# Other shares of the dequantisation levels for three stages of a four-layer kernel on one core

## The chip, the cores and the metric

The kernel runs on one core of a Trainium2 chip. The metric is the device time of that core in microseconds (us), the median of several executions. The profile is of one execution, with its own time.

## The reference

The input x is 64 sequences of 32 positions and 512 features, float32. Four layers follow, each `x = x + ffn(cond(x))`:

- Layer 0: a long convolution along the features with a kernel made from state-space parameters, masked by a length, then a product with a 512x512 fp8 weight.
- Layer 1: every sequence is multiplied by one of 16 adapters (512x512, chosen by `itok_B_1_14`), then a gated feed-forward net of hidden width 1376: `silu(x w1') * (x w2')`, times `w3'`. The three weights are first quantised and dequantised.
- Layers 2 and 3: routed low-rank products, a small memory with top-8 selection, a gate, a convolution across positions and a last 512x512 product.

What the change is about is the quantisation in layer 1. In blocks of 64 elements:

```
absmax = max(abs(block)); idx = searchsorted(bounds, block / absmax)   # 15 bounds
weight = NF4_CODE[idx] * absmax
```

## The kernel before, in words

All products are float32 on TensorE; activations lie transposed (512 features as 4 chunks of 128 partitions, 2048 tokens in 4 blocks `tb` of 512 columns). Each engine has its own instruction list, written out by hand, and the engines wait for each other by semaphores. So the order of the work on an engine is the order of the code.

**Dequantisation.** The weights are cut into 15 units (`UNITS`): 11 units of w1 and w2 together (128 rows by 1024) and 4 of w3 (128 by 1408). A unit takes 15 levels, one for each bound, so there are `PARTS` = 225 levels, numbered m; unit u has levels 15u to 15u+14. ScalarE (ACT) compares the raw weights with bound i (L761) and writes one of four `above` buffers; it may run `NAB` = 4 levels ahead of VectorE. VectorE (DVE) adds the step to the unit's accumulator (L1605 for the first level, L1608 for the others). After a unit's last level DVE multiplies by the block maxima (L1614), then TensorE transposes the unit (`turn_unit`, L1029) and ACT copies it out of PSUM (`evac_quant`, L769). Before level 5 of a unit, DVE prepares the next one (`start_unit`: L1579 maxima, L1580 to L1586 normalising). The raw weights of unit u+2 are loaded by SyncE (SP) once ACT has done with unit u (L519 to L526).

**Where the levels run.** They fill gaps between other work of ACT and DVE, by tables that say how many levels have been done after each step: `K_CONV` (16 steps of the convolution), `K_FFN0` (16 products of layer 0, `NF0` levels), `K_AD` (16 adapters, `NAD` levels) and `K_UP` (44 up products of layer 1). Before a step's own work both engines run the levels of its share. Tables before: 8 levels in the convolution, 7 in layer 0's product, 53 among the adapters (3 or 4 each), 154 in the up projection (97 of these in its first 24 steps, so that the units of w1 and w2 are done there), and `LATE` = 3 at the end.

**The work around them.** In layer 0's product TensorE makes 16 products (`p_ffn0`); DVE adds each to X (L1685). After the last one (`d_x1` = 16) DVE, ACT and GpSimd (POOL) copy X into Y, sequences in order of their adapter (L1690, L789, L683, L687). Then TensorE turns unit 0 and goes through the adapters: 22 groups of up to 4 sequences here, each 32 matmul instructions, with the numbers of groups 0, 1, 1, 2, 2, 1, 1, 2, 1, 2, 2, 1, 1, 2, 3, 0 for the adapters 0 to 15; ACT copies each group out (L801), and a group may start only when the group four before it is out. The first up product needs all groups out. `turns_ad` and `turns_up` say after which adapter or up product a unit is turned; both are worked out from the tables. SP loads the weights of adapter a when adapter a-4 is done, and in the last four turns also stores X (`keep`).

In the up projection a product n gives two banks; ACT takes them out (silu and copy, L836, L837; for the last chunk L840, L841), POOL or DVE multiply them (L691; `hidden`, L1706, L1707). Product n waits until product n-2 is out. For four products (`AHEAD`: n = 28, 29, 32, 33) DVE runs `hidden(n)` before the levels of step n.

Of the kernel before, what the change touches and what calls it, by code (L numbers as in the profile page):

```python
# [32 lines left out]
ADAPT = 16  # L33
# [61 lines left out]
def build(nc, A, out):  # L95
    ctx = ExitStack()
    with ctx:
# [259 lines left out]
        for n in """l_zq g_xs a_xs d_nrm m_ready m_used g_nrm d_xs a_rk a_v2 p_rke a_kk g_pad d_wz p_va a_va p_lgt a_lgt l_l3 a_w16 d_ak d_rmx g_x2 l_cst l_s4 l_s5 l_w0 l_u l_x l_len l_ids l_kpz l_kp0 l_kp1 l_kp2 l_kp3 l_dsk g_dsk d_kz l_keep l_back l_strip0 l_strip1 l_strip2 l_strip3 l_strip4 l_raw0 l_raw1 l_wa0 l_wa1 l_wa2 l_wa3 l_late l_prep l_l3w l_aim g_dec g_c p_c10 d_mix a_out1 a_up g_h  # L357
# [13 lines left out]

        LEV = len(BOUNDS)
        PARTS = LEV * NU
        NCV, NF0, NAD, LATE = 8, 7, 53, 3
        UP_A, UP_B = 24, 20
        BANKS0 = [4, 5, 0, 1, 2, 3]
        BANKS_ST = [3, 2, 5, 3]
# [10 lines left out]
        K_CONV = [min(max(g - 1, 0) * 2 // 3, NCV) for g in range(HG)]  # L388
        K_FFN0 = [K_CONV[-1] + (NF0 + NCV - K_CONV[-1]) * (n + 1) // (TB * DC) for n in range(TB * DC)]
        AD_LAST = K_FFN0[-1] + NAD  # L390
        K_AD = [K_FFN0[-1] + (a + 1) * NAD // ADAPT for a in range(ADAPT)]
        W12 = LEV * NH
        K_UP = [AD_LAST - (-(W12 - AD_LAST) * (n + 1) // UP_A) if n < UP_A else
                min(W12 - (-(PARTS - LATE - W12) * (n + 1 - UP_A) // UP_B), PARTS - LATE) for n in range(TB * NH)]
        assert K_UP[-1] == PARTS - LATE and K_AD[-1] == AD_LAST

# [15 lines left out]
        def parts_of(K, i, first=0):  # L412
            return range(K[i - 1] if i else first, K[i])

        def units_between(a, b):

            return [u for u in range(NU) if a < LEV * (u + 1) <= b]

        def turns_ad(a):
            return units_between(K_AD[a - 3] if a >= 3 else K_FFN0[-1], K_AD[a - 2]) if a >= 2 else []  # L420

        def turns_up(n):
            late = units_between(K_AD[-2], PARTS - LATE)
            at = {u: next(i for i in range(TB * NH) if K_UP[i] >= LEV * (u + 1)) + (1 if u >= NU - 2 else 2) for u in late}
            return [u for u in late if min(at[u], TB * NH - 1) == n]
# [63 lines left out]
        def _(sp):  # L489
# [26 lines left out]
            def load_unit(u):  # L516
                kind, c = UNITS[u]
                if u >= 2:
                    sp.wait_ge(s["m_ready"], 15 * (u - 1))  # L519
                    sp.wait_ge(s[f"l_raw{u % 2}"], 32 * (u // 2))  # L520
                slot = raw[:, u % 2, :]
                got = s[f"l_raw{u % 2}"]
                if kind == 1:
                    h = HCH[c]
                    sp.dma_start(slot[0:h, 0:D], A["w1"][c * P:c * P + h, :]).then_inc(got, 16)
                    sp.dma_start(slot[0:h, D:2 * D], A["w2"][c * P:c * P + h, :]).then_inc(got, 16)  # L526
                else:

                    g, q = c // 2, c % 2
                    o = q * (2 * HID - HALF)  # L530
                    for k in range(2):
                        cols = slice(k * HALF // 2, (k + 1) * HALF // 2)
                        sp.dma_start(slot[:, cols], A["w3"][g * P:(g + 1) * P, o + cols.start:o + cols.stop]
                                     ).then_inc(got, 16)
# [28 lines left out]
            def keep(tb):  # L563
                sp.wait_ge(s["d_x1"], TB * DC)
                sp.dma_start(xkeep.ap()[:, :, tok(tb)], X[:, :, tok(tb)]).then_inc(s["l_keep"], 16)
# [19 lines left out]
            for a in range(NWS - 1, ADAPT):  # L585
# [5 lines left out]
                else:  # L591
                    done = sp.value_load(order[0:1, NB + a - NWS + 1:NB + a - NWS + 2], min_val=0, max_val=NGR)
                    sp.wait_ge(s["p_ad"], done + 1)
                    sp.wait_ge(s[f"l_wa{a % NWS}"], WSINC[a % NWS] * (a // NWS))
                    for u in units_between(K_AD[a - NWS - 1] if a > NWS else K_FFN0[-1], K_AD[a - NWS]):
                        load_unit(u + 2)
                load_adapter(a)
                if a >= ADAPT - TB:
                    keep(a - ADAPT + TB)
            for u in units_between(K_AD[-1 - NWS], PARTS):  # L600
                if u + 2 < NU:
# [119 lines left out]
        def _(act):  # L721
# [32 lines left out]
            def level(m):  # L754

                u, i = divmod(m, LEV)
                h, w = unit_shape(u)
                normed(act, u)
                if m >= NAB:
                    act.wait_ge(s["m_used"], m - NAB + 1)  # L760
                nc.scalar.activation(above[0:h, m % NAB, 0:w], raw[0:h, u % 2, 0:w], ACT.Relu,  # L761
                                     scale=STEEP, bias=cst[0:h, C_BND + i:C_BND + i + 1]).then_inc(s["m_ready"], 1)
# [30 lines left out]
            for a in range(ADAPT):  # L793
                for k in parts_of(K_AD, a, K_FFN0[-1]):
                    level(k)
# [1292 lines left out]
```

## Time and profile before

| what | value |
|---|---|
| median of 3 runs | 868.88 us |
| the runs | 865.85, 868.88, 873.6 us |
| the profiled execution | 865.41 us |
| its span | 863.6 us |
| TensorE busy | 825.8 us, 96% of the span |
| VectorE busy | 638.9 us, 74% |
| ScalarE busy | 415.8 us, 48% |
| granted TensorE clock | 1.000 |

The profiled execution's own time is 1.8 us above its span (what lies around the first and the last instruction), and a little under the lowest of the three runs. The three runs lie 7.75 us apart, 0.9% of the time. A line such as L1608 is a line of the kernel. L969 is the helper of nearly all matmuls, so they are told apart by their operands. A float32 matmul stands as two records.

### The profile page before, as it was taken

What the parts mean: (1) busy time and instruction counts of PE and PEld (TensorE: products, weight loads), DVE (VectorE), ACT (ScalarE), POOL (GpSimd) and SP (SyncE); (2) the same over time, 40 slices, a digit from 0 to 9 for tenths busy, and PEclk for the clock granted to TensorE, in tenths of its full rate; (3) what the DMA queues carried; (4) which work ended last, traced back from release to release, by engine and by line L of the source; (5) the groups of instructions that cost most, each with busy time, mean ns of one, the idle gap of its engine ahead of it and who ended that gap; (6) DMA issues with size and microseconds to landing.
All of it is one profiled execution on the core that took longest, in us unless ns stands there. A gap on an engine that the chain in (4) does not pass through costs nothing.

```text
span 863.6 us, 10782 instructions
## 1 busy us (share of the span) xinstructions
PE 825.8 (96%) x3325; PEld 459.6 (53%) x3326; DVE 638.9 (74%) x981; ACT 415.8 (48%) x550; POOL 152.7 (18%) x162
## 2 busy tenths in 40 slices
PE   2499899999999999999999999999999999999998
PEld 2498799984444444444344444444455554543443
DVE  7899799969999999998999986343362462458445
ACT  5055188869787787886788730000011232245100
POOL 4100099101122211121122200002402022020000
PEclk9999999999999999999999999999999999999999
DMA  6696157920000001101010030013020000002022
GB/s 208 222 375 226 56 214 229 325 106 24 24 3 23 25 18 35 34 0 35 1 33 0 1 97 1 0 58 138 0 68 1 1 0 1 1 1 50 0 98 98
DMA packets 35151, 61.06 MB, mean 71 GB/s; under 512 B 6170, under 2 KB 8988, under 8 KB 34460
## 3 DMA queue, kind: packets, MB, share of 16 engines
q1 hardware_dynamic: 34232, 60.32, 20.6%
q0 software_dynamic: 352, 0.04, 0.2%
q8 instruction: 26, 0.43, 0.2%
q14 instruction: 25, 0.20, 0.1%
q10 hardware_dynamic: 516, 0.07, 0.0%
HBM read 50.90 MB, written 8.47 MB: 69 GB/s over the span
## 4 chain that ended last, share of the span: by engine, by line
PE 83%; DVE 8%; POOLq 3%; issue 2%; POOL 2%; ACT 1%; DMA 1%; SPq 0%; ACTq 0%; DVEq 0%
PE ps L969 81%; DVE acc L1608 3%; POOLq L685 2%; POOL Yp L687 1%; PE ps L1029 1%; PE ps L1301 1%; DVE W2T L1474 1%; DVE T L1608 1%; DVE W2T L1468 1%; DMA T<-kpad 0%; DVE W2T L1471 0%; DMA W2T<-in_log_dt 0%; DVE raw L1586 0%; DVE amax L1579 0%; POOLq L687 0%
## 5 line engine op out<-in xcount | busy, mean ns | idle before, releaser
L761 ACT ACTIVATE above<-raw,cst 128x1024 uint8<-128x1024 f32 (+2 forms) x225 | 267.8, 1233 | 48.6 <-DVE T L1608 20.0
L1608 DVE SCALAR_TENSOR_TENSOR acc<-above,acc 128x1024 f32<-128x1024 uint8 (+2 forms) x112 | 159.6, 1425 | 14.7 <-ACT above L761 11.4
L969 PE MATMUL ps<-Up,W2T 128*128 128x512 f32 (+1 forms) x404 | 160.6, 593 | 0.0
L969 PE MATMUL ps<-Up,W1T 128*128 128x512 f32 x344 | 155.5, 594 | 2.6 <-DVE Up L1707 2.2
L1608 DVE SCALAR_TENSOR_TENSOR T<-above,T 128x1024 f32<-128x1024 uint8 (+1 forms) x84 | 129.4, 1540 | 3.4 <-ACT above L761 0.5
L969 PEld LDWEIGHTS ps<-Up,W2T 128*128 128x128 f32 (+1 forms) x404 | 66.5, 177 | 86.4 <-issue 86.4
L969 PEld LDWEIGHTS ps<-Up,W1T 128*128 128x128 f32 x344 | 64.1, 190 | 81.6 <-issue 76.3
L969 PE MATMUL ps<-Yp,W3T 128*128 (+3 forms) x618 | 104.5, 322 | 1.6 <-POOL Yp L683 1.2
L969 PEld LDWEIGHTS ps<-Yp,W3T 128*128 128x128 f32 (+1 forms) x618 | 79.2, 192 | 23.1 <-issue 22.5
L969 PE MATMUL ps<-X,W3T 128*128 128x512 f32 (+2 forms) x184 | 78.7, 579 | 0.0
L969 PE MATMUL ps<-X,W2T 128*128 128x512 f32 x140 | 61.3, 594 | 0.0
L969 PEld LDWEIGHTS ps<-X,W3T 128*128 128x128 f32 (+1 forms) x184 | 34.1, 190 | 42.6 <-issue 41.0
L1748 DVE TENSOR_TENSOR Yp<-Yp,ps 128x512 f32<-128x512 f32 x14 | 9.3, 684 | 54.0 <-PE ps L969 53.9
L969 PE MATMUL ps<-Up,W3T 128*128 128x256 f32 (+4 forms) x202 | 45.6, 381 | 0.0
L969 PEld LDWEIGHTS ps<-X,W2T 128*128 128x128 f32 x140 | 26.3, 190 | 31.9 <-issue 31.6
L687 POOL COPY Yp<-X x44 | 40.9, 981 | 1.7 <-issue 1.7
L969 PE MATMUL ps<-W1T,W2T 128*128 128x512 f32 (+1 forms) x144 | 36.0, 436 | 4.8 <-DVE W2T L1551 4.8
L691 POOL TENSOR_TENSOR Yp<-Yp 128x512 f32<-128x512 f32 x13 | 18.8, 1442 | 118.8 <-ACT Yp L837 118.8
L711 POOL TENSOR_TENSOR X<-X,Yp 128x2048 f32<-128x2048 f32 x4 | 18.1, 4528 | 121.8 <-ACT Yp L890 121.8
L969 PEld LDWEIGHTS ps<-Up,W3T 128*128 128x128 f32 (+1 forms) x202 | 32.0, 191 | 12.3 <-issue 11.0
L691 POOL TENSOR_TENSOR X<-X,Yp 128x512 f32<-128x512 f32 x15 | 23.5, 1565 | 79.0 <-ACT X L837 79.0
L1901 DVE TENSOR_TENSOR Up<-Up,ps 128x512 f32<-128x512 f32 x4 | 2.8, 688 | 40.6 <-PE ps L1258 40.6
(344 smaller groups left out, 977.1 us busy)
## 6 DMA issues: line engine op xcount, KB each, us to landing
W3T<-in_wa SPq DMA_DIRECT2D x8, 1024.0 KB, 7.2
raw<-in_w SPq DMA_DIRECT2D x20, 256.0 KB, 3.0
W3T<-kpad SPq DMA_DIRECT2D x9, 512.0 KB, 8.5
Up<-in_xconv SPq DMA_DIRECT2D x4, 1024.0 KB, 8.7
X<-in_xT SPq DMA_DIRECT2D x4, 1024.0 KB, 9.7
W1T<-in_wa SPq DMA_DIRECT2D x4, 1024.0 KB, 7.6
xkeep<-X SPq DMA_DIRECT2D x4, 1024.0 KB, 10.6
X<-xkeep SPq DMA_DIRECT2D x4, 1024.0 KB, 9.4
```

Of the source, the lines that this page charges most:

```text
L685: bs = [pool.value_load(order[0:1, bass.ds(t * 4 + i, 1)], min_val=0, max_val=NB - 1) for i in range(4)]
L687: pool.tensor_copy(Y[:, :, bass.ds(t * (4 * S) + i * S, S)], X[:, :, bass.ds(b * S, S)]).then_inc(s["g_xs"], 1)
L691: nc.gpsimd.tensor_tensor(slots[UPS[n]], slots[UPS[n]], sg[n % 2], ALU.mult).then_inc(s["g_h"], 1)
L711: nc.gpsimd.tensor_tensor(X[:, :, tok(tb)], X[:, :, tok(tb)], Y[:, :, tok(tb)], ALU.add).then_inc(s["g_xc"], 1)
L761: nc.scalar.activation(above[0:h, m % NAB, 0:w], raw[0:h, u % 2, 0:w], ACT.Relu, scale=STEEP, bias=cst[0:h, C_BND + i:C_BND + i + 1]).then ...
L969: return nc.tensor.matmul(o, l, r, start=start, stop=stop, **kw)
L1029: last = nc.tensor.transpose(dst, src, ident[0:h, 0:h])
L1301: last = nc.tensor.transpose(ps[:, BANKS_ST[t], c * P:(c + 1) * P], Y[:, c, tile(tb, t)], ident)
L1468: link(V.tensor_tensor(o, a, b, op))
L1474: link(V.scalar_tensor_tensor(out=o, in0=a, scalar=x, in1=b, op0=op0, op1=op1))
L1608: V.scalar_tensor_tensor(out=ac, in0=src, scalar=float(STEPS[i]), in1=ac, op0=ALU.min, op1=ALU.add).then_inc(s["m_used"], 1)
L1748: V.tensor_tensor(o, a, b, op).then_inc(s["d_mix"], 1)
```

## The change

The tables get other sizes. Layer 0's product takes 10 levels in place of 7. The adapters take 57 in place of 53: the first 12 share 41 evenly (3 or 4 each), the last four take 4, 4, 5 and 3. What is left for the up projection is 147 levels in place of 154: its first 24 steps take 90 in place of 97, and from step 23 on `K_UP` is as it was.

```
-        NCV, NF0, NAD, LATE = 8, 7, 53, 3
+        NCV, NF0, NAD, LATE = 8, 10, 57, 3
+        AD_END = [4, 4, 5, 3]
...
-        K_AD = [K_FFN0[-1] + (a + 1) * NAD // ADAPT for a in range(ADAPT)]
+        AD_EVEN = NAD - sum(AD_END)
+        K_AD = [K_FFN0[-1] + ((a + 1) * AD_EVEN // (ADAPT - 4) if a < ADAPT - 4 else AD_EVEN + sum(AD_END[:a + 5 - ADAPT]))
+                for a in range(ADAPT)]
```

Worked out from the tables: the shares in layer 0's product were 0 0 1 0 1 0 1 0 0 1 0 1 0 1 0 1 and are 0 1 0 1 1 0 1 1 0 1 0 1 1 0 1 1. Unit 0 was finished at product 15 and is finished at product 11. The shares among the adapters were 3 3 3 4 3 3 4 3 3 4 3 3 4 3 3 4 and are 3 3 4 3 4 3 3 4 3 4 3 4 4 4 5 3. Units 1, 2 and 3 were turned after the adapters 6, 11 and 15 and are turned after 5, 9 and 14. Units 4 to 9 were turned after the up products 3, 7, 10, 14, 18, 22 and are turned after 2, 5, 9, 13, 17, 21; later units as before.

## Rows read from the trace of the kernel before

**Rows 1.** The page: busy time of the engines, and the chain that ended last.
```profile
PE 825.8 (96%) x3325; PEld 459.6 (53%) x3326; DVE 638.9 (74%) x981; ACT 415.8 (48%) x550; POOL 152.7 (18%) x162
PE 83%; DVE 8%; POOLq 3%; issue 2%; POOL 2%; ACT 1%; DMA 1%; SPq 0%; ACTq 0%; DVEq 0%
```

**Rows 2.** Waits of PE, whole span: total us, times, longest us.
```profile
PE ps L969 <- DMA Yp<-in_l3aT: 14.6, 1, 14.6
...
PE ps L969 <- DVE Up L1707: 2.2, 1, 2.2
```

**Rows 3.** Timeline of DVE, end of layer 0's product: start, us.
```profile
102.57 0.75 DVE L1685 SCALAR_TENSOR_TENSOR X<-ps,wsc,X 128x512 f32<-128x512 f32 x1 [0.48 <-PE ps L969]
103.24 1.22 DVE L1608 SCALAR_TENSOR_TENSOR acc<-above,acc 128x1024 f32<-128x1024 uint8 x1
104.48 1.23 DVE L1614 TENSOR_TENSOR acc<-acc,amax 128x1024 f32<-128x1024 f32 x1
105.75 0.75 DVE L1685 SCALAR_TENSOR_TENSOR X<-ps,wsc,X 128x512 f32<-128x512 f32 x1
```

**Rows 4.** Timeline of PE at the same place.
```profile
105.77 1.09 PE L1029 MATMUL ps<-cst,acc 128*128 128x128 f32 x8 [1.43 <-DVE acc L1614]
108.06 4.48 PE L969 MATMUL ps<-Yp,W3T 128*128 x38 [1.21 <-POOL Yp L683]
```

**Rows 5.** Busy time by stretch: layer 0's product, the adapters.
```profile
74.00:105.00 31.00, 30.34 (x137) 24.92 (x135) 24.41 (x31) 9.93 (x10) 0.00 (x0) 1.00 0.34 119
...
109.00:190.00 81.00, 80.62 (x719) 80.19 (x719) 71.15 (x67) 64.09 (x74) 42.78 (x51) 1.00 0.66 228
```

**Rows 6.** Timeline of DVE among the adapters and behind them.
```profile
109.49 0.86 DVE L1605 TENSOR_SCALAR W2T<-above 128x1024 f32<-128x1024 uint8 x1 [1.03 <-ACT above L761]
...
115.62 1.22 DVE L1579 TENSOR_REDUCE amax<-raw 128x16 f32<-128x1024 f32 x1
...
118.84 12.57 DVE L1608 SCALAR_TENSOR_TENSOR W2T<-above,W2T 128x1024 f32<-128x1024 uint8 x10
...
179.05 0.69 DVE L1605 TENSOR_SCALAR acc<-above 128x1024 f32<-128x1024 uint8 x1
...
191.76 1.23 DVE L1608 SCALAR_TENSOR_TENSOR acc<-above,acc 128x1024 f32<-128x1024 uint8 x1 [6.95 <-ACT above L761]
```

**Rows 7.** Timeline of ACT, last group out and first up product out.
```profile
190.02 0.60 ACT L801 ACTIVATE Up<-ps x1 [2.98 <-PE ps L969]
190.52 4.26 ACT L761 ACTIVATE above<-raw,cst 128x1024 uint8<-128x1024 f32 x4
...
204.29 0.59 ACT L837 ACTIVATE Yp<-ps 128x512 f32<-128x512 f32 x1
```

**Rows 8.** Timeline of PE in the up projection and at its end.
```profile
204.94 3.70 PE L969 MATMUL ps<-Up,W1T 128*128 128x512 f32 x8 [0.26 <-ACT Yp L837]
...
428.35 3.70 PE L969 MATMUL ps<-Up,W1T 128*128 128x512 f32 x8 [2.16 <-DVE Up L1707]
...
508.97 1.39 PE L1029 MATMUL ps<-cst,acc 128*128 128x128 f32 x11 [0.70 <-issue]
```

**Rows 9.** Timeline of DVE around the products taken ahead, and the last unit.
```profile
398.22 0.68 DVE L1706 TENSOR_TENSOR Yp<-Yp,ps 32x512 f32<-32x512 f32 x1 [3.23 <-ACT Yp L841]
...
427.61 0.69 DVE L1707 TENSOR_TENSOR Up<-Yp,ps 64x512 f32<-64x512 f32 x1
...
502.27 4.94 DVE L1608 SCALAR_TENSOR_TENSOR acc<-above,acc 128x1408 f32<-128x1408 uint8 x3 [2.89 <-ACT above L761]
```

**Rows 10.** DMA: a load of raw weights by SP; the stores of X.
```profile
175.83 0.35 SPq L525 DMA_DIRECT2D raw<-in_w  x1
```
```profile
xkeep<-X SPq DMA_DIRECT2D x4, 1024.0 KB, 10.6
```

**Rows 11.** DVE groups by form: adapters (first), up projection (second).
```profile
L1608 DVE SCALAR_TENSOR_TENSOR acc<-above,acc 128x1024 f32<-128x1024 uint8 x15 | 18.4, 1225 | 1.8 <-ACT above L761 1.3
```
```profile
L1608 DVE SCALAR_TENSOR_TENSOR T<-above,T 128x1024 f32<-128x1024 uint8 x42 | 60.0, 1430 | 1.4
```

## The prediction

> **What bounds the kernel now.** I read the page first. TensorE is busy for 96% of the span, and the chain that ended last runs through it for 83% [rows 1]. The granted clock was 1.00 throughout. So time can only be won where TensorE waits, or where its matmuls start further apart than they need to, and it can be lost wherever it is made to wait anew. The view of PE's waits then says how much there is. The largest wait, 14.6 us, stands before the first matmul that needs a load at the very start and has nothing to do with the levels [rows 2]. From the convolution on none is longer than the 2.2 us for DVE's L1707 [rows 2]. The timelines of PE show where these waits are, and what else is near the stages that the change touches:
>
> - Before unit 0 is turned: 1.43 us, until L1614 is done; right behind it 1.21 us until X has been copied for the first group [rows 4].
> - Before the third up product: 0.26 us, for ACT's L837 [rows 8].
> - Before up product 34: 2.16 us, for DVE's L1707 [rows 8].
> - Before the last unit is turned: 0.70 us [rows 8].
>
> These make 5.8 us, 0.7% of the time, and that is all that any placing of the levels could bring. A busy DVE or ACT is no cost here by itself: DVE's 74% matters at those places alone.
>
> **Layer 0's product, three levels more.** The end of this stage is the first term. DVE adds product 14 to X at 102.57, then runs level 14 (1.22 us) and closes unit 0 with L1614 (1.23 us), and only at 105.75 adds product 15 [rows 3]. TensorE had finished product 15 at 105.77 - 1.43 = 104.34 [rows 4]. Two things hang on this: the turning of unit 0 (the 1.43 us), and the copies of X, which wait for all 16 additions. The turn, 1.09 us long, covers part of the second wait. What sets the first group's start at 108.06 is the addition at 105.75, 2.31 us before it [rows 3, 4].
>
> After the change, unit 0 is closed at product 11. Behind product 14's addition stands one ordinary level, m = 17, and no L1614. Adding product 15 can thus start at 102.57 + 0.67 + 1.24 = 104.5, if product 14 is not taken sooner; the steps in the rows are 103.24 - 102.57 = 0.67 and 104.48 - 103.24 = 1.24. Product 14's row has an idle time of 0.48 before it that ended with PE, so it can't be sooner. Because level 16 now stands before product 14 as well, and its predecessor has none, I allow 0.1 to 0.2 us on top of this: 104.6 to 104.7 against 105.75. The gain is 105.75 - 104.65 = **1.1 us**. The turn of unit 0 moves up by more than that and stops being felt.
>
> Is there room for the three levels? DVE is busy 24.41 us of the 31 us from 74 to 105 [rows 5]. Two of the added levels are of 1.24 us and one, the first of unit 1, is a cheaper L1605; together at most 3.7 us, against 6.6 us of idle time. ACT is busy 9.93 us of 31 [rows 5] and has room for three more. The load of unit 2's raw weights stays where it is in SP's order, before adapter 3, and what it waits for comes earlier. So this part costs nothing while there is cover; without the cover it would be 1.24 us a level. Six PSUM banks stand between TensorE and a late addition, so it takes a backlog of several products before that is felt.
>
> **Adapters, four levels more.** TensorE is busy 80.62 us of 81 here [rows 5]. The stage ends when its 22 groups are done and out; it does not wait for DVE. I follow DVE, because ACT may be only four levels ahead of it, and ACT's copying out of a group stands behind the levels of that adapter's share. A level takes 12.57 / 10 = 1.257 us, and preparing a unit 118.84 - 115.62 = 3.22 us [rows 6]. With the first level at 0.73 and closing at 1.26 a unit takes 0.73 + 14 x 1.257 + 3.22 + 1.26 = 22.8 us. DVE starts with m = 18 at about 108.3 (before, m = 15 at 109.49 [rows 6], less the 1.1 us). Two levels, a preparation, ten levels and the closing make 19.6 us, so unit 1 is done at 127.9, unit 2 at 150.7 and unit 3 at 173.5. Before, they were turned at 136.7, 167.0 and 189.5; now, after adapters 5, 9 and 14, at about 132, 154 and 188. The smallest reserve is about 3 us, at unit 2, so the moved turns cost nothing.
>
> The end of the stage is tighter. Adapter 14's share ends with m = 71, which ACT can make only when DVE has used m = 67. From 173.5: five levels of unit 4 (5.8), the preparation of unit 5 (3.2) and three levels (3.8) lead to 186.3. ACT's level takes 1.07 us (4.26 / 4 [rows 7]), to 187.4, and then two groups that have been waiting go out at 0.5 us each, to 188.4. TensorE, 1.1 us earlier than before, ends its last group at 189.5 - 1.1 = 188.4 and turns unit 3 until 189.3. The last group goes out meanwhile. So the reserve is about nothing. My formula for a unit gives 68.4 us for the three units of before, and DVE took 179.05 - 109.49 = 69.6 us for them [rows 6]. With half of this difference I put a new wait of **0.5 us** at the start of the up projection; its bounds are 0 (DVE as by the formula) and 2 us (DVE short by all of that difference, and a load arriving late, the rival below). Before, DVE stood idle for 6.95 us at this very place [rows 6], because ACT had its last four levels behind the last group, at 190.52 [rows 7]. These 6.95 us are what pays for the four levels on DVE, and they are why so little is lost.
>
> For SP, the loads of units 3, 4 and 5 move up by one to two adapters or so. In front of adapter 7's and adapter 11's weights SP now waits for the end of units 1 and 2 on ACT, by my count for 1 to 2 us. Those weights are needed 13 us or more after their issue; even a store of that size takes only 10.6 to land [rows 10], so this is covered.
>
> **Up projection, seven levels fewer.** Steps 0 to 23 have 90 levels in place of 97. The 0.26 us before the third product go: ACT has four levels ahead of product 0 instead of five, and those of adapter 15 are three, not four. It was done with L837 at 204.29 + 0.59 [rows 7]; two levels fewer are at least 2.1 us. Gain **0.3 us**. The rest of the seven levels comes off a DVE that no one waits for. At product 28 DVE is idle for 3.23 us until ACT has handed it the product [rows 9]. So whatever DVE is ahead by is lost there: it starts again at 398.22 (less the shift), with the same list of work, because `K_UP` is unchanged from step 23 on. The 2.16 us at product 34 arise only behind this point, from 398.22 to 427.61 + 0.69 without a pause to speak of [rows 8, 9]. They stay. The 0.70 us before the last unit stay too: DVE waits 2.89 us for ACT before its last three levels, and ACT for TensorE's last up product [rows 9].
>
> The rows also show a level at 1.225 us among the adapters and at 1.430 us in the up projection, for the same shape [rows 11]. The Trainium skill (SBUF — State Buffer, "Who interferes with whom") says that a DVE operation with two SBUF inputs and a GpSimd operation that reads SBUF exclude each other, and that the later one blocks. The trace agrees with that, since POOL multiplies beside DVE in the up projection. By the rule, seven levels cost DVE 7 x 1.430 = 10.0 us where they were and 7 x 1.225 = 8.6 us where POOL is idle; as DVE's lead is lost at product 28, the time is the same by either.
>
> **The sum.** -1.1 (handing over X) - 0.3 (third product) + 0.5 (start of the up projection) = -0.9 us. Against the profiled execution that is 865.41 - 0.9 = 864.5 us (span 862.7). The four executions shown, 865.41 to 873.6, have their middle at 867.4; the forecast for a median of runs is 867.4 - 0.9 = **866.5 us**.
>
> **Rivals.**
>
> 1. *The stall at product 34 goes too.* This would be so if the idle time at product 28 were not where DVE's lead is lost, for instance if ACT handed it over sooner because its ring of levels is freer. For it: DVE is the releaser of that wait. Against it: the 3.23 us, and an unchanged table. Time: 866.5 - 2.2 = 864.3. Chance 0.08.
> 2. *Nothing arrives.* The first group is held by something that doesn't move with the additions, such as GpSimd's start; or the wait at the start of the up projection is 1.4 us and eats both gains. For it: the reserve worked out above is near nothing. Time: 867.4. Chance 0.2.
> 3. *Slower: the end of the adapters.* The raw weights of unit 5 were issued at 175.83 [rows 10] and used 17 us later. Now DVE wants them at 179.3, while SP issues them at about 169, behind the last store of X, and such a store takes 10.6 us to land [rows 10]: 166.5 + 10.6 = 177.1, and 2 to 3 us for the weights themselves, 179 to 180. If they are late, DVE, ACT's level 71, the last groups and TensorE's first up product are late by as much. It decides from 1.4 us on; at 3 us the sum is -1.4 + 3 = +1.6, so 869.0. Chance 0.1.
> 4. *The change doesn't do what it says*, because ACT in fact still makes the last levels behind the last group: then the up projection starts as before and the gain is 1.4 us, time 866.0. Chance 0.05, hardly told from the forecast.
>
> The forecast itself has 0.57.
>
> **How the numbers follow.** All of these cases lie within 3.1 us of 867.4, which is 0.4%. A measurement of this kernel tells a change from no change from about 1% on; its runs are themselves 0.9% apart. So within 1%: 0.96; faster 0.02, slower 0.02, for a cause that I have not seen. The range has to take in the rivals, from 864.3 to 869.0, and the scatter of a median, for which I take about half the distance of the runs shown, 2 to 3 us on either side: 862 to 871.5.
>
> **What would show each step right or wrong.** Right: in the timeline of DVE the last L1685 of layer 0's product at 104.6 or so, with L1608 and not L1614 before it; PE's wait for L1614 gone and its first adapter matmul at about 107.0; the wait for L837 near 204 gone; DVE's idle time of 7 us at the end of the adapters gone, and that before product 28 grown from 3.23 us to around 10; PE's 2.2 us for L1707 still there. Wrong: a PE wait of over 1.4 us for ACT's L801 at the start of the up projection, an idle DVE before an L1579 near 179, or a PE wait inside the adapters before a turn (L1029) or for weights. If the 2.2 us for L1707 is gone, rival 1 is right.

## The result, and the profile after

| | before | changed |
|---|---|---|
| median, 20 runs each | 867.11 us | 869.36 us |
| lowest to highest | 865.43 to 873.6 us | 866.81 to 871.82 us |
| profiled execution (span) | 865.41 (863.6) us | 871.28 (869.5) us |
| mean granted clock in it | 1.000 | 0.995 |

The ratio is 1.0023, with a 95% interval of 1.0013 to 1.0034. The change makes the kernel slower by about 2 us, where 0.9 us less were forecast. The size is within the 1% forecast; the side is not.

The page of the changed kernel says little beside [rows 1]. TensorE has 3.7 us more busy time in as many instructions, which is a first sign that some of them ran at the lower clock:

```profile
PE 829.5 (95%) x3325; PEld 462.4 (53%) x3326; DVE 631.6 (73%) x981; ACT 414.7 (48%) x550; POOL 157.3 (18%) x162
```

All lines of the changed kernel behind the tables are those of before plus 3 (`e4` plus 5, `e8` plus 4): L1608, L1611 and L1617 are the first level, the others and the closing; L1688 adds a product to X, L1032 turns a unit, and L804, L1710 and L1582 stand for L801, L1707 and L1579. POOL's copy of X is L686 (before L683).

**Handing over X.** The timeline of DVE at the end of layer 0's product, which answers to [rows 3]:

```profile
98.53 1.23 DVE L1617 TENSOR_TENSOR acc<-acc,amax 128x1024 f32<-128x1024 f32 x1
99.79 0.75 DVE L1688 SCALAR_TENSOR_TENSOR X<-ps,wsc,X 128x512 f32<-128x512 f32 x1
102.16 0.69 DVE L1608 TENSOR_SCALAR W2T<-above 128x1024 f32<-128x1024 uint8 x1 [1.62 <-issue]
102.89 1.41 DVE L1688 SCALAR_TENSOR_TENSOR X<-ps,wsc,X 128x512 f32<-128x512 f32 x2
104.22 1.22 DVE L1611 SCALAR_TENSOR_TENSOR W2T<-above,W2T 128x1024 f32<-128x1024 uint8 x1
105.47 0.75 DVE L1688 SCALAR_TENSOR_TENSOR X<-ps,wsc,X 128x512 f32<-128x512 f32 x1
106.14 1.22 DVE L1611 SCALAR_TENSOR_TENSOR W2T<-above,W2T 128x1024 f32<-128x1024 uint8 x1
107.39 0.75 DVE L1688 SCALAR_TENSOR_TENSOR X<-ps,wsc,X 128x512 f32<-128x512 f32 x1
```

And the timeline of PE at the same place, which answers to [rows 4]:

```profile
105.48 1.03 PE L1032 MATMUL ps<-cst,acc 128*128 128x128 f32 x8
109.61 6.11 PE L972 MATMUL ps<-Yp,W3T 128*128 x38 [3.10 <-POOL Yp L686]
```

The reader is to see four things. L1617 is done early, as meant, so the turn starts without a wait. The last L1688 nevertheless starts at 107.39, 1.75 us after TensorE's last matmul of layer 0 had ended (105.25 + 0.39 = 105.64); before it started at 105.75, 1.41 us after that. DVE was idle for 1.62 us before level 15 and waited for nothing that the profile names ("issue"). And the two waits of 1.43 and 1.21 us, with 1.09 us of turning between them [rows 4], have become one of 3.10 us, behind which the same 38 records take 6.11 us, not 4.48.

The whole layer stands 1.3 us later in this execution. 0.9 us of it is that TensorE waited 4.1 us for the convolution's strips instead of 3.2 (waits for T from kpad). That is ahead of the change, so stages are compared from the start of the last matmul of layer 0's product on: 103.95 before, 105.25 here. From there to the first group it was 4.11 us and is 4.36.

**The clock.** Busy time by stretch (us, PE, PEld, DVE, ACT, POOL, PEclk, DMA share, GB/s) of the changed kernel, at the first adapters and at one place in layer 3:

```profile
104.00:110.00 6.00, 2.90 (x19) 2.37 (x18) 5.67 (x12) 1.72 (x6) 1.59 (x7) 1.00 0.46 158
110.00:114.00 4.00, 4.00 (x24) 4.00 (x23) 2.92 (x4) 4.00 (x4) 4.00 (x9) 0.57 0.86 291
114.00:118.00 4.00, 4.00 (x38) 4.00 (x37) 3.83 (x6) 2.67 (x4) 2.69 (x6) 1.00 0.44 119
...
822.00:828.00 6.00, 6.00 (x16) 2.46 (x17) 5.89 (x10) 0.00 (x0) 0.00 (x0) 0.72 0.23 86
```

Before, the four microseconds from 110 hold 38 records at a granted 1.00; here they hold 24 at 0.57, because for 3.4 us of them (110.1 to 113.5) the clock is at the lower of its two levels, 1.2 GHz instead of 2.4 (granted 0.50). TensorE is busy for all of the stretch in both kernels, so no wait shows this loss. It costs 6.11 - 4.48 = 1.6 us.

**End of the adapters.** Timelines of ACT and of PE there, which answer to [rows 7, 8]:

```profile
188.64 3.67 ACT L764 ACTIVATE above<-raw,cst 128x1024 uint8<-128x1024 f32 x3 [3.17 <-DVE acc L1611]
192.30 0.60 ACT L804 ACTIVATE Up<-ps  x1
193.53 0.60 ACT L804 ACTIVATE Up<-ps  x1 [0.63 <-PE ps L972]
194.75 0.60 ACT L804 ACTIVATE Up<-ps  x1 [0.63 <-ACT Up L804]
```

```profile
193.04 1.04 PE L1032 MATMUL ps<-cst,T 128*128 128x128 f32 x8
195.40 3.70 PE L972 MATMUL ps<-Up,W1T 128*128 128x512 f32 x8 [1.33 <-ACT Up L804]
...
432.52 3.70 PE L972 MATMUL ps<-Up,W1T 128*128 128x512 f32 x8 [2.14 <-DVE Up L1710]
```

There is the new wait, of 1.33 us where 0.5 was put down. ACT's levels are in front of the last groups now, and the groups go out 1.23 us apart. The 2.14 us at product 34 are still there. DVE's timeline answers to [rows 6, 9]:

```profile
184.11 1.22 DVE L1582 TENSOR_REDUCE amax<-raw 128x16 f32<-128x1024 f32 x1 [1.73 <-DMA raw<-in_w]
...
197.47 3.74 DVE L1611 SCALAR_TENSOR_TENSOR acc<-above,acc 128x1024 f32<-128x1024 uint8 x3 [1.36 <-ACT above L764]
...
402.42 0.68 DVE L1709 TENSOR_TENSOR Yp<-Yp,ps 32x512 f32<-32x512 f32 x1 [6.44 <-ACT Yp L844]
```

The 6.95 us before the last levels are 1.36 now, and those at product 28 have grown from 3.23 to 6.44. DVE also waits 1.73 us for the raw weights of unit 5.

**The sum of the two profiled executions** (span 869.5 against 863.6), by the start times in PE's timelines:

| stretch | before | changed | difference |
|---|---|---|---|
| start to last matmul of layer 0's product | 103.95 | 105.25 | +1.3, of it 0.9 at the strips |
| from there to the first group | 4.11 | 4.36 | +0.25 |
| first group to first up product | 82.62 | 85.79 | +3.17: 1.3 wait, 1.6 clock, 0.2 small gaps |
| up start to third up product | 14.26 | 13.84 | -0.42 |
| from there to the end | 658.66 | 660.26 | +1.6: a second 3.4 us at 0.50, from 823.5 |

In the stretches of the first and the last row no wait grew that the change touches, so they are not laid to it. The rest is +3.0 us in one execution, in which the lower clock and the wait at the end of the adapters happened to stand together. Whether they always do was the first thing to ask.

### The profile page after: what moved, and what is told of

The parts are those of the page before. It is cut to its first block, busy times and chain, and to the rows that moved or that the text cites. A ratio compares the mean times of both kernels' runs of the same rounds, so it can differ in the third digit from the quotient of the medians.

```text
span 869.5 us, 10782 instructions
## 1 busy us (share of the span) xinstructions
PE 829.5 (95%) x3325; PEld 462.4 (53%) x3326; DVE 631.6 (73%) x981; ACT 414.7 (48%) x550; POOL 157.3 (18%) x162
## 4 chain that ended last, share of the span: by engine, by line
PE 87%; DVE 8%; DMA 1%; issue 1%; ACT 1%; SPq 0%; DVEq 0%; ACTq 0%; POOL 0%; POOLq 0%
PE ps L972 85%; DVE acc L1611 2%; PE ps L1032 1%; DMA T<-kpad 1%; PE ps L1304 1%; DVE W2T L1477 1%; DVE T L1611 1%; DVE W2T L1471 1%; DVE X L1688 0%; DVE W2T L1474 0%; DMA W2T<-in_log_dt 0%; DVE amax L1582 0%; DVE W2T L1611 0%; DVE W2T L1527 0%; DVE raw L1638 0%
## 5 line engine op out<-in xcount | busy, mean ns | idle before, releaser
L764 ACT ACTIVATE above<-raw,cst 128x1024 uint8<-128x1024 f32 (+2 forms) x225 | 263.9, 1232 | 26.6 <-DVE acc L1611 13.1
L1611 DVE SCALAR_TENSOR_TENSOR acc<-above,acc 128x1024 f32<-128x1024 uint8 (+2 forms) x112 | 158.4, 1414 | 12.7 <-ACT above L764 9.6
L1611 DVE SCALAR_TENSOR_TENSOR T<-above,T 128x1024 f32<-128x1024 uint8 (+1 forms) x84 | 125.0, 1488 | 9.4 <-ACT above L764 6.5
L972 PE MATMUL ps<-Yp,W3T 128*128 (+3 forms) x618 | 106.4, 325 | 3.4 <-POOL Yp L686 3.1
L839 ACT ACTIVATE Yp<-ps 128x512 f32<-128x512 f32 x40 | 23.7, 593 | 49.7 <-PE ps L972 49.7
L694 POOL TENSOR_TENSOR Yp<-Yp 128x512 f32<-128x512 f32 x13 | 22.6, 1736 | 115.9 <-ACT Yp L840 115.9
```

The costliest lines, as they stand in the source:

```text
L694: nc.gpsimd.tensor_tensor(slots[UPS[n]], slots[UPS[n]], sg[n % 2], ALU.mult).then_inc(s["g_h"], 1)
L839: nc.scalar.activation(sg[n % 2][0:h, :], ps[0:h, n % 2, :], ACT.Silu).then_inc(s["a_silu"], 1)
L972: return nc.tensor.matmul(o, l, r, start=start, stop=stop, **kw)
L1611: V.scalar_tensor_tensor(out=ac, in0=src, scalar=float(STEPS[i]), in1=ac, op0=ALU.min, op1=ALU.add).then_inc(s["m_used"], 1)
```

## The experiments

There are three sets, each on a chip of its own and beside its own runs of the kernel before: `a1` to `e3` (35 runs of before, median 867.48 us), `e4` to `e7` (29 runs, 868.07 us) and `e8` to `e10` (29 runs, 867.92 us). The ratios are against these.

### The changed kernel again

No edit; the profile and the runs are taken once more.

> The changed kernel once more, for a second profile. Its profiled execution had TensorE wait 3.1 us before the first adapter group and then a granted clock of 0.5 for 3.4 us, which put 1.6 us between the starts; if the clock falls because of that wait, this profile shows the same fall at the same place, and 1.002 of the time of before (+2 us). If the fall was an accident of that execution, it is absent here and the changed kernel stays slower by no more than 1 us.

Measured: 870.65 us in 12 runs, 1.0036 (1.0021 to 1.0050). PE waits 3.19 us before the first group. Behind it the clock is at 0.50 for 6.8 us from 108.5, and TensorE waits only 0.16 us before the up projection. Without that wait it took 85.44 us from the first group to there (before 82.62), so it had lost 2.8 us, and ACT was no longer behind. So the lower clock returns at the same place, and it and the new wait partly replace each other. DVE waits only 0.44 us for unit 5's raw weights in this profile, against 1.73 us in the first.

### Layer 0's part alone

```
-        NCV, NF0, NAD, LATE = 8, 7, 53, 3
+        NCV, NF0, NAD, LATE = 8, 10, 50, 3
```

> Ten levels in layer 0's product, 50 among the adapters, so that the up projection is as before. Theory A (the change loses at the handing over of X, through a late last addition and a fall of the clock): +1.5 to +2 us, a wait of about 3 us before the first adapter group and the half clock behind it. Rival B (the loss is at the end of the adapters, where DVE finds the weights of unit 5 not there): 0 to -1 us here.

Measured: 868.25 us, 1.0013 (0.9994 to 1.0032). The stretch from the last matmul of layer 0 to the first group is 4.46 us (before 4.11), and the clock is at 0.50 from 108.0 to 114.8. The part that was to bring 1.1 us brings nothing. Theory A had said +1.5 to +2; the medians differ by 0.8 us, and the interval takes in 0. The profile has no wait for a group at the start of the up projection.

### The adapters' part alone

```
-        NCV, NF0, NAD, LATE = 8, 10, 57, 3
+        NCV, NF0, NAD, LATE = 8, 7, 57, 3
```

> Seven levels in layer 0's product and the change's 57 among the adapters. Theory A: little, -0.4 to +1 us (the wait for L837 goes, some wait for ACT's last group comes). Rival B: +1.5 to +2 us.

Measured: 867.08 us, 0.9998 (0.9985 to 1.0011). The hand-over is as before, 4.11 us, with its two waits of 1.42 and 1.21 us. In the profiled execution the clock still fell, from 108.8 on for 3.4 us. So it can fall behind the two waits as well. The four levels by themselves cost nothing measurable. But this is not the whole of the change's second part: with 7 levels in layer 0's product all levels among the adapters are numbered 3 lower, so ACT has level 68 and not 71 in front of the last groups, and the profile has no wait for a group at the start of the up projection. The wait of 1.33 us needs both parts of the change.

### DVE's register loads four products earlier

The loads in question read from `order` which sequences DVE is to copy. They stand in front of product 12:

```
-                if n == (TB - 1) * DC:
+                if n == (TB - 2) * DC:
                     first = [dve.value_load(order[0:1, i:i + 1], ...) for i in range(GX)]
```

> The changed kernel with DVE's three register loads of L1683 at product 8, not 12. In the changed kernel they take 1.6 us of DVE's list where it had just closed unit 0, and the three levels behind them then delay the last addition to 1.9 us after TensorE's last matmul of layer 0. Theory A: the last addition comes 1.0 us or more sooner against TensorE, the wait before the first group shrinks from 3.1 to about 2 us, and if the clock then stays at 1.00 the kernel is 2 to 2.7 us faster than the changed one (about 0 or -0.5 us against before). Rival (the backlog is made by the levels alone, not by these loads): no difference to the changed kernel.

Measured: 867.19 us, 1.0004 (0.9987 to 1.0021). The question was where the 1.62 us of "issue" before level 15 come from. In the changed kernel the trace has these loads on DVE's sequencer at 99.8 to 101.3, right there (ns min/median/max, first and last start):

```profile
L1683 DVEq TENSOR_LOAD <-order x3: 298/305/566, 99.8 to 101.3; - x3
L1683 DVEq FUSED_REGOPS  x3: 183/190/216, 100.4 to 101.7; - x3
```

With them moved, the timeline of DVE in `e3` is:

```profile
98.99 0.68 DVE L1608 TENSOR_SCALAR W2T<-above 128x1024 f32<-128x1024 uint8 x1
99.71 1.63 DVE L1688 SCALAR_TENSOR_TENSOR X<-ps,wsc,X 128x512 f32<-128x512 f32 x2
101.25 1.22 DVE L1611 SCALAR_TENSOR_TENSOR W2T<-above,W2T 128x1024 f32<-128x1024 uint8 x1
102.50 0.75 DVE L1688 SCALAR_TENSOR_TENSOR X<-ps,wsc,X 128x512 f32<-128x512 f32 x1
103.17 1.21 DVE L1611 SCALAR_TENSOR_TENSOR W2T<-above,W2T 128x1024 f32<-128x1024 uint8 x1
104.42 0.75 DVE L1688 SCALAR_TENSOR_TENSOR X<-ps,wsc,X 128x512 f32<-128x512 f32 x1
```

and PE's, first group and first up product:

```profile
106.65 4.48 PE L972 MATMUL ps<-Yp,W3T 128*128 x38 [1.60 <-POOL Yp L686]
...
190.63 1.55 PE L972 MATMUL ps<-Up,W1T 128*128 128x512 f32 x3 [1.29 <-ACT Up L804]
```

The hole is gone, the last addition starts at 104.42, and the first group starts 2.87 us after layer 0's last matmul: 1.24 us less than before. That is the gain that was forecast (1.1). The clock stayed at 1.00 throughout this profile. On the same chip `e3` is 3.5 us faster than `a1`, and it is back at the time of the kernel before. The wait at the end of the adapters is untouched, and ACT's timeline of `e3` shows how it is made:

```profile
183.87 3.67 ACT L764 ACTIVATE above<-raw,cst 128x1024 uint8<-128x1024 f32 x3 [1.69 <-DVE acc L1611]
187.53 0.60 ACT L804 ACTIVATE Up<-ps  x1
188.75 0.60 ACT L804 ACTIVATE Up<-ps  x1 [0.63 <-PE ps L972]
189.98 0.60 ACT L804 ACTIVATE Up<-ps  x1 [0.63 <-ACT Up L804]
```

Level 71 is done at 187.53, where 187.4 was forecast. Three groups stand behind it and leave 1.23 us apart, though one copy takes 0.60 us. Between two copies ACT's loop has a register load (0.28 us in the trace), its register operation (0.15 us) and short loop instructions. They are out at 190.58, and TensorE starts at 190.63.

### The loads moved without the change

The same edit as `e3`, made in the kernel before.

> The kernel before with DVE's three register loads at product 8, nothing else. In the kernel before these loads lie where DVE waits for TensorE and no level stands right behind them, so by theory A they cost nothing there: 0, at most -0.5 us. If they are worth 1 us or more here too, e3's gain over the changed kernel is a gain of its own and does not explain why the change lost.

Measured: 867.78 us, 1.0000 (0.9986 to 1.0015). DVE has idle time there in the kernel before, and the loads lie in it: its trace has them starting at 97.3 to 98.8, between the additions at 97.23 and 99.42, with no level behind them. If they delay the second addition a little, nothing of it is left at product 14, before which DVE waits 0.48 us for TensorE [rows 3]. So `e3`'s gain over the changed kernel is no saving of its own; the loads cost something only once levels fill that idle time.

### Unit 5's raw weights ahead of the last store of X

```
-                if a >= ADAPT - TB:
+                if ADAPT - TB <= a < ADAPT - 1:
                     keep(a - ADAPT + TB)
...
                 if u + 2 < NU:
                     load_unit(u + 2)
+                if i == 0:
+                    keep(TB - 1)
```

> The changed kernel with the last store of X behind the load of unit 5's raw weights in SP's order. In the changed kernel's profile DVE waited 1.7 us for that load. Theory C (that late load makes the wait for ACT at the start of the up projection): the DVE wait goes, the up projection starts 1.2 us sooner after the first adapter group, and the kernel is about 1 us faster than the changed one. Rival D (the wait at the start is made by the five levels in front of adapter 14's three groups and by ACT's own pace of 1.23 us a group): no difference, since e3 showed 1.3 us of this wait with no DVE wait for a load.

Measured: 868.99 us, 1.0023 (1.0008 to 1.0037), the changed kernel's own ratio. In the changed kernel's first profile DVE waited 1.73 us for this load; in `e4` it does not. The profile has what theory C said. Behind the same 3.4 us at 0.50 (109.8 to 113.2) TensorE waits for no group at the start of the up projection:

```profile
192.51 0.60 ACT L806 ACTIVATE Up<-ps  x1 [0.87 <-PE ps L974]
193.16 3.70 PE L974 MATMUL ps<-Up,W1T 128*128 128x512 f32 x8
```

From the first group to there it takes 84.40 us, against 85.79 in the changed kernel's first profile, so 1.39 us less. In that profile it was thus the late load that left the wait of 1.33 us standing beside the clock's loss. The median doesn't show this gain against the changed kernel's 1.0023; against `a1`'s 1.0036 (1.0021 to 1.0050) `e4` is about 1 us lower, which these intervals don't settle. Rival D is right with the clock full: in `e3` DVE goes into L1582 at 179.34 without a wait, and PE's wait is 1.29 us all the same. Two ways meet at the first up product, TensorE's own and the one through DVE's levels, ACT's level 71 and the groups' way out, and only the later one counts.

### The wait filled with work

24 transposes of the identity into a bank that is free, behind the turn of unit 0. They compute nothing that is used.

```
+            pe.wait_ge(s["d_x1"], TB * DC - 2)
+            for i in range(24):
+                nc.tensor.transpose(ps[:, 4, i % 4 * P:(i % 4 + 1) * P], ident, ident)
```

> The changed kernel with 24 more transposes of the identity into a free bank on TensorE, 2.6 us of it, in the wait between unit 0's transposes and the first adapter group. They compute nothing that is used. Theory A (the wait makes the granted clock fall behind it): the half clock near 110 us goes, and the kernel is 1.5 to 2.5 us faster than the changed one though it does more. Rival (the fall has nothing to do with the wait): the half clock stays and the time is that of the changed kernel, or up to 0.5 us more.

Measured: 868.60 us, 1.0007 (0.9991 to 1.0024). PE's timeline and the busy time by stretch:

```profile
105.37 2.78 PE L1076 MATMUL ps<-cst 128*128 128x128 f32 x24
108.63 4.49 PE L972 MATMUL ps<-Yp,W3T 128*128 x38 [0.47 <-POOL Yp L686]
```

```profile
110.00:114.00 4.00, 4.00 (x38) 4.00 (x38) 3.78 (x4) 4.00 (x5) 3.94 (x8) 1.00 0.72 259
```

The first group starts as late as in the changed kernel, 4.36 us after layer 0's last matmul. But the 38 records take 4.49 us again at a granted 1.00. It is the idle 3.1 us, not the late start, that the lower clock follows.

The time gained is less than the 1.5 to 2.5 us expected: on the same chip it is 0.4 us in the medians (0.6 in the means) below `e4`, whose profile has the lower clock. The reason stands at the end of the adapters. With the clock full TensorE comes there earlier and waits 0.82 us for the last group, and from the first group to the up projection it takes 84.00 us, only 0.40 less than in `e4`.

### The turn behind the group, in the kernel before

The same long wait, made in the kernel before without any level moved: unit 0 is turned behind adapter 1's group.

```
-            turn_unit(0)
...
+                if a == 1:
+                    turn_unit(0)
```

> The kernel before, with unit 0's transposes behind adapter 1's group and not in front of it. TensorE then waits in one piece, about 3.7 us, from its last matmul of layer 0 to the first group, and the work is the same. By the waits alone: 0 (the transposes move from inside the wait to behind a group) to +0.9 us. With theory A: the half clock follows the wait, in most executions, and adds 1.6 us or more: +2 to +3 us and a mean clock below that of before.

Measured: 872.47 us in 6 runs, 1.0051 (1.0032 to 1.0069). PE's timeline and the stretches:

```profile
108.25 6.55 PE L969 MATMUL ps<-Yp,W3T 128*128 x32 [3.63 <-POOL Yp L683]
```

```profile
104.00:110.00 6.00, 2.37 (x11) 1.97 (x10) 4.40 (x10) 0.71 (x3) 2.95 (x12) 0.76 0.56 191
110.00:114.00 4.00, 4.00 (x21) 4.00 (x21) 0.00 (x0) 0.00 (x0) 1.54 (x7) 0.50 0.67 243
```

One wait of 3.63 us takes the place of 1.43 + 1.09 + 1.21 us, and the clock is at 0.50 from 107.2 to 114.0. The 1.0 us of turning comes in addition, less the 0.1 by which the group is earlier, so 0.9 of the 4.4 us are work. Its profile has 2.9 us for the lower clock in the first groups (half of the 5.76 us from 108.25 to 114.01) and a new wait of 0.60 us for a group to be taken out, at 134.15.

### Three levels before adapter 14, five before 15

`e3`, with two levels moved from adapter 14's share to adapter 15's, so that ACT makes one level and not three ahead of the waiting groups.

```
-        AD_END = [4, 4, 5, 3]
+        AD_END = [4, 4, 3, 5]
```

> e3 (register loads at product 8) with the last four adapters' shares 4, 4, 3, 5 in place of 4, 4, 5, 3. Rival D above: ACT has two levels fewer in front of the last three groups, the wait of 1.3 us at the start of the up projection goes, and the kernel is 1.0 to 1.3 us faster than e3, so 1 to 1.8 us faster than before. Theory C: no difference to e3.

> The kernel of e6 once more, beside e8 on one chip: 0.998 to 0.999 of the time of before, as measured at first.

Measured: 866.60 us, 0.9986 (0.9975 to 0.9997), and in a second set of 12 runs on another chip 866.12 us, 0.9983 (0.9972 to 0.9995). ACT's timeline of the first:

```profile
184.90 1.15 ACT L764 ACTIVATE above<-raw,cst 128x1024 uint8<-128x1024 f32 x1 [2.04 <-DVE acc L1611]
186.03 0.60 ACT L804 ACTIVATE Up<-ps  x1
187.26 0.60 ACT L804 ACTIVATE Up<-ps  x1 [0.63 <-ACT Up L804]
189.86 0.60 ACT L804 ACTIVATE Up<-ps  x1 [2.00 <-PE ps L972]
```

Before the last group out ACT now waits 2.00 us for TensorE, not the other way round, and TensorE goes from the turn into the up projection at 190.51 without a wait. This beats the kernel before, by 1.5 and 1.8 us in the medians of the two sets (1.2 and 1.5 us by the ratios), as expected.

### The stall at product 34 as well

`e6`, with two levels of unit 12's run held back at products 31 and 32, and unit 13 turned one product later.

```
+        K_UP[31], K_UP[32] = 186, 189
...
-            at = {u: ... + (1 if u >= NU - 2 else 2) for u in late}
+            at = {u: ... + 2 for u in late}
...
-            pe.wait_ge(s["a_qt"], QB[W3_FIRST + 2])
+            pe.wait_ge(s["a_qt"], QB[W3_FIRST + 3])
```

> e6 with two levels fewer before up product 32 (K_UP[31] = 186, K_UP[32] = 189, from step 33 on as it was), so that DVE comes to the hidden product 32 on time, and with unit 13 turned after product 41. The wait of 2.2 us at product 34 should go, and with it the half clock that follows it in some executions: 1.5 to 3 us faster than e6, so about 3 to 4 us faster than before. Rival: DVE is busy without a pause from product 28 to the last levels, so the 2.2 us only come back as a wait at the turn of unit 12 or 13, or before the last unit; then the same as e6.

Measured: 865.97 us, 0.9973 (0.9960 to 0.9986), the lowest of the study. But 1.5 to 3 us less than `e6` were expected, and `e10`, the same kernel as `e6` on the same chip, has 866.12: 0.15 us in the medians, 0.6 us in the means, and the intervals overlap. The 2.16 us of L1710 (in `e6`) are gone, and over half of them comes back as two smaller waits in PE's timeline:

```profile
440.79 3.70 PE L973 MATMUL ps<-Up,W1T 128*128 128x512 f32 x8 [0.87 <-ACT Up L841]
...
508.16 1.39 PE L1033 MATMUL ps<-cst,acc 128*128 128x128 f32 x11 [1.18 <-issue]
```

1.18 stands where 0.70 stood [rows 8], so the net of these waits is 2.16 - 0.87 - 0.48 = 0.8 us. From the first up product to the wait of 0.95 us in layer 3 the profiles of `e8` and `e10` differ by 0.5 us (626.11 against 626.62). The rival, that most of it comes back, is nearer to this than the forecast.

### How often the clock fell

Every execution has its mean granted clock. At full clock throughout it is 0.999 or more; one stretch of 3.4 us at 0.50 takes 3.4 x 0.5 / 864 = 0.002 from it and costs 1.6 us, so 0.001 of it is 0.8 us. Over all runs on record, each against the mean of its kernel and set, 0.001 less goes with 0.73 us more. Up to 0.001 of a mean can come from behind the last matmul, where the lower clock costs nothing.

| kernel | wait(s) before the first group, us | runs at 0.999 or more | mean clock |
|---|---|---|---|
| before, with its turn between | 1.43 and 1.21 | 35 of 93 | 0.9981 to 0.9984 by set |
| changed and `a1` | 3.1 | 1 of 32 | 0.9966, 0.9950 |
| `e1` | 3.19 | 3 of 12 | 0.9969 |
| `e2` | 1.42 and 1.21 | 3 of 12 | 0.9973 |
| `e3` | 1.60 | 6 of 12 | 0.9981 |
| `e4` | 3.1 | 0 of 12 | 0.9961 |
| `e5` | 0.47 | 6 of 12 | 0.9984 |
| `e6` and `e10` | 1.69 | 7 of 24 | 0.9982 (`e6`) |
| `e7` | 3.63 | 0 of 6 | 0.9940 |
| `e8` | 1.6 | 3 of 12 | 0.9983 |
| `e9`, with its turn between | 1.42 and 1.16 | 4 of 12 | 0.9978 |

The kernels with one wait of 3.1 us or more, not filled, have the five lowest means; `e2`, which has the two short waits, comes close behind with 0.9973. A mean below 0.999 doesn't say where the clock fell: of the runs of before 58 have one too. The changed kernel's 0.9966 against 0.9982 is 0.0016, or about 1.3 us. Its single run at full clock took 866.81 us, against a median of 865.9 to 866.3 us, by set, for the runs of before at full clock. `e5`, with the changed kernel's starts, has six runs at full clock with a median of 867.96 us, 1.7 us above those of before in its set.

## Why the prediction was wrong

Its forecast was -0.9 us from three terms. The profiles give +0.25 to +0.35 for handing over X and -0.42 for the third up product. The stretch between them, from the first group to the first up product, took 82.62 us before. It is +1.4 with the clock full (`e5`, 84.00), +1.8 with one fall of the clock and the load on time (`e4`, 84.40), +3.0 with a fall of 6.8 us (`a1`, 85.60) and +3.2 with a fall of 3.4 us and a late load (changed, 85.79). The sums are +1.2, +1.6, +2.9 and +3.0 us. The two medians of the changed kernel are 2.25 and 3.17 us above before. So what the lower clock costs and the new wait can't be added: each takes the place of the other, unless the load is late too. The clock had no term in the prediction.

- **"Handing over X: -1.1"** is the step that failed; it measured +0.25. The sum for DVE counted levels, closings and additions, and left out what the code of that loop issues besides: three register loads in front of product 12, some 2 us of DVE's list. "So this part costs nothing while there is cover" was checked over the whole stage (24.41 of 31 us [rows 5]); what had to be followed were the last four products, where unit 0's closing, the loads and the levels from 15 on follow each other. `e3` takes away the loads and gets -1.24; `e9` shows that before they were covered.
- **"The turn of unit 0 moves up by more than that and stops being felt"** was true of its start and wrong in what was drawn from it. The turn was also what stood between two waits [rows 4]. Without it there is one wait of 3.1 us, and the lower clock behind it in both profiles; 31 of the 32 runs have a mean clock below 0.999, against 58 of 93 before. `e5`, with the wait filled and the start left late, and `e7`, with the wait made in the kernel before, show this from both sides. The prediction read "the granted clock was 1.00 throughout" off one execution and took it for granted; it is so in 35 of 93 runs.
- **"Start of the up projection: +0.5"**: the mechanism was right, the size was not. It measured 1.3 us at full clock (`e3`), less when the clock has held TensorE back (0.16 in `a1`, none in `e4`). ACT's level 71 came as forecast in `e3`, at 187.53 against 187.4; the term mis-sized is "two groups that have been waiting go out at 0.5 us each". They were three, 1.23 us apart. The duration of one L801 in [rows 7] is not the step of the loop it stands in. The upper bound, 2 us, held.
- **Third up product: -0.3**: it measured -0.42.
- **What pays for four more levels**: as forecast, DVE's idle 6.95 us went (1.36 are left), its lead was lost at product 28, where it is idle 6.44 us (about 10 forecast), and the waits at product 34 and before the last unit stayed. No turn inside the adapters waited. `e2` has these four levels at no cost, though with three fewer in front of them.
- **A reading that nothing hung on:** seven levels at 1.225 us each "where POOL is idle". POOL was busy for 42.78 of the 81 us among the adapters [rows 5]; from 111 to 153 us it copied X, and the 14 levels into W2T in that time took 1.23 us each. So the rows don't show that a level is faster there because POOL is idle, and the agreement claimed rests on the up projection alone.
- **The rivals.** Rival 3 (slower, unit 5's load, 869.0 us) came true in part. The wait is there, 1.73 us on DVE in one profile of the changed kernel and 0.44 in the other, and in the first it costs 1.4 us, set beside `e4`'s profile. It is not the main cause: `e4` without it is still 1.0023, `e1`, which has no wait for a group at this end, still has the lower clock, and `e3` recovers the whole loss with its edit in layer 0's product. That the time came near to 869.0 is in part luck. Rival 1 did not happen; `e8` shows that it takes a change of `K_UP` and is worth about 0.5 us in place of 2.2. Rival 2's second half (a wait of 1.4 us at the up projection eating the gain) is nearest to what happened at that place, but the gain it was to eat had never arrived. In rival 4 ACT was to make the last levels behind the last group, and it does not.

"Within 1%" and the range held; they were wide enough for a change of the wrong sign. What stays open is why, of executions of one program with the same waits, some show the lower clock behind them and some not: the profile names the wait ahead of each such stretch, but not what decides. How much of the median is the late load, and the 0.2 us of small gaps among the adapters of the changed kernel, were not isolated either.

## What to carry to other kernels

Cover is counted in the last few steps before a hand-over, not over the stage, and from the code of the loop: register loads and everything else it issues belong to the sum, though no busy time shows them. Before work that stands between two waits of TensorE is moved away, the two are to be added to the one that will be left, and a way looked for to shorten or fill it. Where two ways meet, as TensorE's and ACT's do at the first up product, a loss on one hides a loss on the other: taking away one of them gives back only the difference (0.4 us in `e5`). Where single microseconds count, the mean granted clock of many runs is read beside their times; one profile at 1.00 says nothing of the others.

## What the runs showed of the hardware

- **Where the clock falls.** In every profile of the study each stretch at 0.50 while TensorE had work began within 1.5 us of the end of a wait of TensorE (1.1 us before it to 1.5 us behind it) and lasted 3.4 or 6.8 us. At the first group it came with the waits of 3.1 to 3.6 us in all profiles that have them (changed, `a1`, `e1`, `e4`, `e7`), and with 1.42 and 1.21 us, parted by the turn, in `e2` but not in the kernel before or `e9`. With one wait of 1.60 to 1.69 us (`e3`, `e6`, `e8`, `e10`) it did not come there. At product 34, behind 2.15 us, it came in five of the twelve profiles that have the wait (`a1`, `e1`, `e2`, `e4`, `e6`). In layer 3 it came behind 0.95 us (823.5 in the changed kernel) in seven of thirteen. The Trainium skill (TensorE: Matmul & The Clock Gate, "Why this matters for your kernels") asks for no long gaps between bursts of matmuls. The trace agrees for the wait at the first group; that the clock also fell behind the 0.95 us in layer 3 goes beyond it.
- **The start of a profile.** Up to 35 us TensorE has its longest waits (14.6, 4.8, 2.8 and 3.2 us before), and the view gives a granted clock of 1.00 there. But the trace has no record of the clock before 38.0 us in the kernel before (40.7 in `e10`), and the records of one product come at 11 in the 3.4 us from 34.8 and at 23 in the 3.0 us from 38.2. So it is likely, not shown, that the clock was at the lower level until then too. The same 32 records take 6.55 us before, 6.80 in the changed kernel and up to 8.03 (`e10`), which makes single executions differ ahead of the change.
- **A register load is not free for an engine that computes.** Each took 0.30 to 0.57 us plus 0.18 to 0.22 for its register operation on DVE's sequencer, and DVE stood idle for 1.62 us beside the three. On ACT a loop of one such load (0.28 us plus 0.15) and one copy of 0.60 us per group stepped at 1.23 us.
